# The gates' turn and spread moved from TensorE to VectorE block transposes and DMA reads, GELU in place in four PSUM banks

## The reference

```
h = layernorm(x) * (1 + ca) + sa
Q, K = elu(h Wq + bq) + 1, elu(h Wk + bk) + 1;  V = h Wv + bv        # 16 heads of 16
x = x + ga * (Q (K^T V) / (Q sum(K)) Wo + bo)
h = layernorm(x) * (1 + cb) + sb
logits = (h/|h|) . (centroids/|centroids|) + h . w_route              # 8 experts a token
gates  = softmax over the two largest logits, 0 for the other six
x = x + gb * sum_e gates[e] * (gelu(h w1[e] + b1[e]) w2[e] + b2[e])   # each expert 256 -> 128 -> 256
```

## Time and profile before

| | |
|---|---|
| median of three runs | 405.95 us |
| profiled execution: span from first to last instruction | 403.2 us (no other time of this execution is given; the median lies 2.75 us above it) |
| TensorE matmul busy | 377.8 us, 94% |
| TensorE weight load busy | 353.0 us, 88% |
| VectorE busy | 321.6 us, 80% |
| GpSimd busy | 285.1 us, 71% |
| ScalarE busy | 213.0 us, 53% |
| mean granted clock of TensorE | 0.987 of full |
| DMA | 13.44 MB, mean 33 GB/s |

### The profile page before, as it was taken

The page is one execution under the profiler, slowest core; times in us unless marked ns, Lnnn a source line. Parts: engine busy times, 40 slices in busy tenths (PEclk is TensorE's granted clock), DMA queues, the critical chain, the costliest instruction groups (busy, mean ns, idle before and its releaser), DMA issues.

```text
span 403.2 us, 9271 instructions
## 1 busy us (share of the span) xinstructions
PE 377.8 (94%) x2834; PEld 353.0 (88%) x2834; DVE 321.6 (80%) x880; ACT 213.0 (53%) x467; POOL 285.1 (71%) x263
## 2 busy tenths in 40 slices
PE   3999999999896759999999999999999999999995
PEld 3568889889775649999999999999999999999995
DVE  5998888888779887888888788888887888766644
ACT  2357877877552244453644644545545546455442
POOL 5426888788675768778878797797797877857410
PEclk9999999999999689999999999999999999999999
DMA  7954000000000000000000000000000000000000
GB/s 274 331 164 125 2 0 0 0 0 2 1 2 0 0 1 2 28 2 27 2 26 26 0 26 18 8 26 2 26 26 0 26 26 0 27 12 18 26 28 27
DMA packets 13706, 13.44 MB, mean 33 GB/s; under 512 B 1106, under 2 KB 12658, under 8 KB 13684
## 3 DMA queue, kind: packets, MB, share of 16 engines
q1 hardware_dynamic: 12868, 12.12, 9.6%
q10 hardware_dynamic: 816, 1.05, 0.8%
HBM read 8.98 MB, written 4.19 MB: 33 GB/s over the span
## 4 chain that ended last, share of the span: by engine, by line
PE 74%; DVE 11%; POOL 5%; issue 5%; DMA 2%; ACT 1%; SPq 0%; DVEq 0%; POOLq 0%
PE bank L698 19%; PE bank L700 19%; PE bank L699 18%; PE bank L706 4%; PE bank L909 3%; PE bank L762 2%; PE bank L869 2%; DMA x_sb<-in_x 2%; PE bank L877 2%; PE bank L927 2%; PE bank L730 2%; POOL hid_lo L470 1%; PE bank L795 1%; DVE stats L1034 1%; POOL early L443 1%
## 5 line engine op out<-in xcount | busy, mean ns | idle before, releaser
L470 POOL TENSOR_TENSOR hid_lo<-hid_g,hid_hi 128x512 fp32r<-128x512 f32 x56 | 72.1, 1288 | 39.9 <-ACT hid_hi L651 38.8
L642 ACT ACTIVATE hid<-bank,cols_sb 128x256 f32<-128x256 f32 x128 | 53.7, 470 | 76.7 <-PE bank L700 76.7
L698 PE MATMUL bank<-tr_hi,w_hi 128*128 128x256 f32 x256 | 73.6, 287 | 0.0
L698 PE MATMUL bank<-w_hi,hid_hi 128*128 128x256 f32 x252 | 71.5, 284 | 0.5 <-POOL hid_lo L470 0.5
L700 PE MATMUL bank<-tr_hi,w_lo 128*128 128x256 f32 x256 | 71.9, 281 | 0.0
L699 PE MATMUL bank<-tr_lo,w_hi 128*128 128x256 f32 x256 | 71.9, 281 | 0.0
L699 PE MATMUL bank<-w_lo,hid_hi 128*128 128x256 f32 x252 | 70.3, 279 | 0.0
L700 PE MATMUL bank<-w_hi,hid_lo 128*128 128x256 f32 x252 | 70.2, 279 | 0.0
L651 ACT ACTIVATE hid_hi<-hid_g 128x512 fp32r<-128x512 f32 x64 | 40.5, 632 | 44.0 <-DVE hid_g L1309 44.0
L1309 DVE TENSOR_TENSOR hid_g<-hid,bank 128x512 f32<-128x512 f32 x64 | 43.9, 686 | 21.8 <-ACT hid L642 21.5
L476 POOL TENSOR_TENSOR g_exp<-euler,shifted 128x16 f32<-128x16 f32 x16 | 49.2, 3077 | 5.2 <-DVE shifted L1342 4.6
(11 more groups left out here) (159 smaller groups left out, 989.3 us busy)
## 6 DMA issues: line engine op xcount, KB each, us to landing
x_sb<-in_x SPq DMA_DIRECT2D x16, 256.0 KB, 2.8
out<-x_sb SPq DMA_DIRECT2D x15, 256.0 KB, 2.1
early<-in_wmod ACTq DMA_DIRECT2D x2, 512.0 KB, 7.6
q_sb<-in_w SPq DMA_DIRECT2D x2, 512.0 KB, 6.5
q_sb<-in_w SPq DMA_DIRECT2D x1, 1024.0 KB, 9.5
q_sb<-in_wqkvT SPq DMA_DIRECT2D x1, 768.0 KB, 6.3
early<-in_wmod SPq DMA_DIRECT2D x1, 512.0 KB, 4.1
wo_sb<-in_woT SPq DMA_DIRECT2D x1, 256.0 KB, 7.5
```

The lines of the kernel that those rows point to most:

```text
L470: gp.tensor_tensor(hid_lo[:, s, :, :], hid_g[:, s, :, :], hid_hi[:, s, :, :].bitcast(F32), ALU.subtract).then_inc(e_hlo, 1)
L642: last = ac.activation(hid[:, s, j, :], bank[2 + s][:, 2 * P * j:2 * P * (j + 1)], ACT.Gelu, bias=b1_sb[:, e:e + 1])
L698: te.matmul(out_ap, l_hi, r_hi, start=start, stop=False)
```

## The change

The gates of unit u+1 no longer pass TensorE after `route`. Four VectorE block transposes (32 × 32 blocks) turn the logits inside bank 1, four more turn the finished gates from tokens on partitions to experts on partitions (`gT_f`, 32 partitions). SP writes the eight rows of gates (8 KB) to DRAM scratch `g_dram` and reads them back in two DMAs, each four experts' rows to all 128 partitions (512 KB to SBUF), into `g_bc`. VectorE multiplies the GELU's result, now left in its own PSUM bank, with `g_bc`. `first` uses four banks (2 to 5) instead of two, `hid_hi` and `hid_lo` get four buffers. Only the second largest's power is taken on GpSimd (2 values a partition instead of 16). Logit work tensors lie in PSUM. The centroids' norms are folded into the routing weights in phase A. The order of every engine's step is rewritten: `second(u, 2)` and `second(u, 3)` come in step u+1, `route(u+2)` comes last in step u.

```diff
@@ SP
+            def put_gates(u):
+                wait(sp, e_gT, u.count(1, 1))
+                sp.dma_start(g_dram[u.h, :, :], gT_f[3 * NE:4 * NE, u.h, :]).then_inc(g_put, 16)
+            def spread_gates(u, k):
+                if k == 0:
+                    wait(sp, g_put, u.count(16, 16))
+                wait(sp, e_mul, u.count(NP, 2 * k + 2 - NP))
+                of = g_dram[u.h, 4 * k:4 * k + 4, :].rearrange("(p j) n -> p j n", j=2)
+                sp.dma_start(g_bc[:, 2 * k:2 * k + 2, :, :], of.partition_broadcast(P)).then_inc(g_got[k], 16)
+            def step_e(u):
+                n = u.plus(1)
+                if n:
+                    put_gates(n)
+                    spread_gates(n, 0)
+                if u.plus(-1):
+                    store(u.plus(-1))
+                if n:
+                    spread_gates(n, 1)
@@ GpSimd: order of a step is now lo_e(u-1, 3), exp_gates(u+1), lo_e(u, 0), make_prod(u+4), lo_e(u, 1),
@@ lo_e(u, 2), add_experts(u-1), norm_e(u+2), rstd_e(u+3), make_qz(u+4)
             def norm_e(u):
+                gp.tensor_scalar(h_n2[:, u.h, :], h_n2[:, u.h, :], NORM_EPS2, None, ALU.max).then_inc(e_n2, 1)
...
             def exp_gates(u):
-                gp.tensor_tensor(g_exp[:, :, :].rearrange("p t e -> p (t e)"), euler[:, :],
-                                 shifted[:, :, :].rearrange("p t e -> p (t e)"), ALU.pow).then_inc(e_gexp, 1)
+                gp.tensor_tensor(second_by[:, :], top[:, :, 1], top[:, :, 0], ALU.subtract).then_inc(e_shift, 1)
+                wait(pool, e_shift, u.count(1, 1))
+                gp.tensor_tensor(g_second[:, :], euler[:, :], second_by[:, :], ALU.pow).then_inc(e_gexp, 1)
@@ ScalarE: gelu(0), hi_o, hi_hid(0), gelu(1), keep_gates(u+1), hi_hid(1), gelu(2), square(u+2), hi_hid(2),
@@ gelu(3), hi_e(u+2), hi_hid(3); keep_logits is gone
             def keep_gates(u):
-                wait(act, e_gTp, u.count(1, 1))
+                wait(act, e_gT, u.count(1, 1))
...
             def gelu(u, p):
-                wait(act, e_mul, u.count(NP, p - 1))
...
-                    last = ac.activation(hid[:, s, j, :], bank[2 + s][:, 2 * P * j:2 * P * (j + 1)], ACT.Gelu,
-                                         bias=b1_sb[:, e:e + 1])
+                    half = bank[2 + p][:, 2 * P * j:2 * P * (j + 1)]
+                    last = ac.activation(half, half, ACT.Gelu, bias=b1_sb[:, e:e + 1])
@@ TensorE (tp_logits, spread_gates, tp_gates are gone)
             def first(u, p):
-                wait(pe, e_gelu, u.count(NP, p - 1))
+                wait(pe, e_mul, u.count(NP, p + 1 - NP))
...
             def step_e(u):
+                first(u, 0); tp_o(u+3); first(u, 1); second(u-1, 2); attend(u+3)       # conditions at both ends left out
+                first(u, 2); second(u-1, 3); first(u, 3); tp_e(u+2); second(u, 0); second(u, 1); route(u+2)
@@ VectorE
             def gate(u, p):
-                wait(dve, e_gb, u.count(NP, p + 1))
+                wait(dve, g_got[p // 2], u.count(16, 16))
-                TT(hid_g[...], hid[...], bank[4 + s][:, :], ALU.mult)
+                TT(hid_g[...], bank[2 + p][:, :], g_bc[:, p, :, :], ALU.mult)
             def gates_a(u):
+                wait(dve, e_route, u.count(1, 1))
+                for q in range(4):
+                    last = ve.transpose(lg[32 * q:32 * (q + 1), :, :], by_quarter[:, :, q, :])
+                # then: cosine part times h_rn (128x32), a reduce to logit, ve.max per tile,
+                # first_of and second_of by is_ge; lg, logit, second_of, g_sel in bank 1
             def gates_b(u):
+                # per tile g_sel = max(second_of * g_second, first_of); reduce; reciprocal; two products
+                # to g_nat; one subtraction g_nat - g_nat
+                for q in range(4):
+                    last = ve.transpose(to, part.bitcast(F32))
+                last.then_inc(e_gT, 1)
             def step_e(u):
+                gates_a(u+1); gate(u, 0); lo_o(u+3); gates_b(u+1); gate(u, 1); modulate_e(u+2)
+                add_attention(u+3); gate(u, 2); scale_experts(u-1); stats_e(u+3); gate(u, 3)
+                denominators(u+4); lo_e(u+2)
@@ set-up: sel, sel_f, fold and their six instructions are gone; in phase A, step 1 of VectorE gets
+                if u.nth(1):
+                    split_b2()        # seven small instructions
+                    split_route()     # waits for GpSimd's cent_rn, three instructions
@@ passage
-            pe.wait_ge(cent_n2_ready, 1)       # tp_a of unit 14
```

More of the change, by code:

```diff
@@ L809, in _ @@
             mod_rows(1)
+            pe.wait_ge(cent_sq_ready, 1)
+            for c in range(NC):
+                last = te.matmul(bank[5][:, 0:NE], ones_f, cent_sq[:, c, :], start=(c == 0), stop=(c == NC - 1))
+            last.then_inc(cent_done, 1)
             pipeline(te, step_a, 1, 2, NU - 4, NU - 3)
@@ L822, in make_m @@
                 last.then_inc(f_m, 1)
-            pe.wait_ge(small_ready, 1)
             pe.wait_ge(a_hf, NU - 3)
-            for c in range(NC):
-                last = te.matmul(bank[0][:, E:E + NE], ones_f, cent_sq[:, c, :], start=(c == 0), stop=(c == NC - 1))
-            last.then_inc(cent_done, 1)
             sum_k(0, bank[0][:, 0:E])
@@ L900, in first @@
                 last.then_inc(e_f1, 1)
-            def spread_gates(u, p):
-                s = p % 2
-                if p == 0:
-                    wait(pe, e_gT, u.count(1, 1))
-                wait(pe, e_mul, u.count(NP, p - 1))
-                for j in range(2):
-                    last = te.matmul(bank[4 + s][:, 2 * P * j:2 * P * (j + 1)], sel[:, 2 * p + j, :], gT[:, u.h, :],
-                                     start=True, stop=True)
-                last.then_inc(e_gb, 1)
             def second(u, p):
-                s = p % 2
                 wait(pe, *lo_made(u, p))
@@ L951, in step_e @@
             def step_e(u):
-                n = u.plus(1)
-                if u:
-                    if not u.nth(0):
-                        first(u, 0)
-                    spread_gates(u, 0)
-                if u.nth(-1):
-                    route(n)
-                    tp_o(u.plus(3))
-                else:
-                    if u.plus(3):
-                        tp_o(u.plus(3))
-                    if n:
-                        route(n)
+                if u and not u.nth(0):
+                    first(u, 0)
+                if u.plus(3):
+                    tp_o(u.plus(3))
+                if u and not u.nth(0):
+                    first(u, 1)
+                if u.nth(-1):
+                    first(u.plus(1), 0)
+                if u.plus(-1):
+                    second(u.plus(-1), 2)
+                if u.plus(3):
+                    attend(u.plus(3))
+                if u.nth(-1):
+                    make_m(1, bank[7])
+                    first(u.plus(1), 1)
+                if u:
+                    first(u, 2)
                 if u.plus(-1):
@@ L990, in step_e @@
                 if u:
-                    second(u, 2)
-                if n:
-                    tp_gates(n)
+                    second(u, 0)
+                    second(u, 1)
+                if u.plus(2):
+                    route(u.plus(2))
             step_a(unit(NU - 2))
@@ new lines, in gates_a, with gates_b @@
+                wait(dve, e_top, u.count(1, 1))
+                TT(first_of[:, :, :], logit, top[:, :, 0:1].to_broadcast([P, 2, NE]), ALU.is_ge)
+                TT(second_of, logit, top[:, :, 1:2].to_broadcast([P, 2, NE]), ALU.is_ge).then_inc(e_gstep, 1)
+            def gates_b(u):
+                wait(dve, e_gstep, u.count(G, 3))
+                wait(dve, e_gexp, u.count(1, 1))
+                for t in range(2):
+                    last = ve.scalar_tensor_tensor(g_sel[:, t, :], second_of[:, t, :], g_second[:, t:t + 1],
+                                                   first_of[:, t, :], ALU.mult, ALU.max)
+                last.then_inc(e_gstep, 1)
```

422 lines of the change are left out of this document (188 added, 234 removed).

## The result

The changed kernel takes 414.76 us (median of four runs, 413.55 to 415.69) against 405.68 us for the kernel before beside it: ratio 1.0221, 95% interval 1.0186 to 1.0256. The forecast was 388.4 us, 378 to 402. The profiled execution has a span of 412.7 us and a time of 414.25, so 1.55 us lie outside the span (2.75 were counted).

What follows compares the result with a forecast made beforehand. VectorE's loop was taken as the bound at 15.1 us a step (3.0 + 9.5 + 2.65). 148.0 us ahead plus 237.6 for the steps and end gave a 385.6 span; with 2.75 added, 388.4 us, range 378 to 402.

Steps and rivals of the forecast that it cites:

- TensorE is the bound before: Steady step of the kernel before: TensorE is busy for all of its 16.01 us, so its list sets the step.
- TensorE's floor of 14.3 us: TensorE's list in a changed step: 16.01 less 1.68 us for gate spreads and the logits' and gates' turns.
- The loop `lo_e`, `route`, `gates_a`, ..., `lo_e`: From one lo_e's end to the next, VectorE's work and the wait for route set the step: 15.1 us.
- The transposes: VectorE's block transposes in gates_a and gates_b: 0.24 us each without overlap, 0.96 for four; bounds 0.12 and 0.38.
- `gates_b`, 2.65 us with blocking: VectorE's work from the two products per tile to the four gate transposes: 2.4 us, plus 0.25 blocking by GpSimd.
- rival (d): No difference: blocking on both comparisons and dear transposes together, 16.3 us a step or more, 403 us and up; chance 0.07.
- VectorE's step without gates, 9.5 us: Gate products, lo_o, add_attention, lo_e, modulate_e (1.6), scale_experts, statistics and denominators on VectorE sum to 9.5 us a step.
- Step 0 like the others: Step 0 was counted among steps 0 to 11 at 15.1 us each, 181.2 us in all.
- The end, 56.4 us: Steps 12 to 15 at 14.3, 12.5 and twice 11.6 us, last matmuls 2.8, then 3.9 to the end.
- Ahead of the steps, +0.3: Start-up, step 1 and passage up to lo_e(1): net +0.6 us, taken as +0.3, so it ends at 148.0.
- The DMAs: Put of the gates about 2.1 us; reads have 9.0 us of room, with 4.1 to 7.6 seen for 512 KB: both fit.
- The 2.75 us between span and median: The median time was taken to lie 2.75 us above the profiled span.

Runs made afterwards that it cites:

- experiment 10: The kernel before the change, with the gates spread over half of the tokens only (output not the reference's): 402.69 us, 0.9921 of the kernel before.
- experiment 12: Experiment 7 with the splits of b2 and of the centroids' columns moved from VectorE's step 1 to behind denominators(0): 390.73 us, 0.9630 of the kernel before.
- experiment 2: The changed kernel with lo_e ahead of denominators on VectorE: 409.63 us, 1.0096 of the kernel before.
- experiment 4: The changed kernel with the four transposes of gates_b done twice, once into a spare tile: 433.44 us, 1.0652 of the kernel before.
- experiment 8: The changed kernel with four more matmuls of 256 columns a step on TensorE: 415.23 us, 1.0236 of the kernel before.
- experiment 1: The changed kernel with modulate_e ahead of gate(u, 1) on VectorE: 417.39 us, 1.0278 of the kernel before.
- experiment 3: The changed kernel with modulate_e ahead of gate(u, 1) and lo_e ahead of denominators on VectorE: 406.42 us, 1.0009 of the kernel before.
- experiment 5: Experiment 3 with gelu(u, 2) ahead of hid_hi(u, 1) on ScalarE: 402.30 us, 0.9909 of the kernel before.
- Experiment 7: Experiments 5 and 6 together, with GpSimd's three add_bo spread over steps -1 and 0: 394.62 us, 0.9737 of the kernel before.
- Experiment 6: Experiment 3 with first(15, 0) ahead of second(14, 0), and scale_experts ahead of lo_hid(u, 2) in the last two steps: 399.99 us, 0.9865 of the kernel before.
- experiment 9: The changed kernel with each read of the gates issued twice, one after the other: 415.79 us, 1.0254 of the kernel before.
- experiment 11: Experiment 7 with make_qz ahead of rstd_e on GpSimd: 401.24 us, 0.9885 of the kernel before.

## Why the prediction was wrong

The spans differ by 412.7 - 385.6 = 27.1 us from the forecast's. By its own parts: `lo_e(1)` ended at 150.17 and not at 148.0 (+2.2); steps 0 to 11 took 196.4 us, from there to 346.55, and not 181.2 (+15.2); the rest took 66.15 us and not 56.4 (+9.8).

*TensorE is the bound before.* Right, by experiment 10.

*TensorE's floor of 14.3 us.* Nearly: 14.92 busy in the changed kernel, with its waits, and 14.46 in experiment 12, with few.

*The loop `lo_e`, `route`, `gates_a`, ..., `lo_e`.* Right in its mechanism, by the idles of 0.75 us on VectorE and 0.5 on TensorE once a step, and by experiments 2, 4 and 8. A second wait of TensorE, 0.7 us a step before `second(u, 0)`, was not foreseen; experiment 8 shows that it cost nothing in the steady step.

*The transposes.* Right: 0.24 us each in `gates_b`, 0.27 in `gates_a`, no overlap.

*`gates_b`, 2.65 us with blocking.* Right: 269.79 to 272.48, 2.69. The comparisons on the logits' bank were not blocked (0.17 us each), so rival (d), with blocking there and dear transposes, is not what happened, though the time came out where it put it. (Its condition was also mispriced: two comparisons at 1 us each are 15.1 + 2.0 - 0.2 = 16.9 us a step, not 16.)

*VectorE's step without gates, 9.5 us.* **This is the step that failed.** It took `modulate_e` as 1.6 us, as in the earlier trace rows, in a place where it now starts together with a GpSimd instruction that reads SBUF: 2.62 us. The forecast asked of every *new* instruction what GpSimd does beside it, and of no *moved* one. In the step shown that alone is the difference: forecast 3.0 + 9.5 + 2.65 = 15.15, measured 16.03 from end to end, of which +1.02 `modulate_e`, +0.16 the lead to the first gate, -0.3 the rest. Every second step is 0.5 us longer (16.52): its first gate waits 0.40 us for a GELU, and L1296 takes 0.60. Eleven steps at 16.24 instead of 15.1 are 12.5 of the 15.2 us, and `modulate_e` at 1.0 us each is 11.4 of them. Taking that microsecond away did not by itself give it back: experiment 1 gained nothing, the same move on top of experiment 2 gave 3.2 us (experiment 3), and only with the GELU moved too (experiment 5) was the step 15.12 us.

*Step 0 like the others.* It took 17.7 us (149.54 to 167.28), the other 2.6. A wait of 0.81 us for `g_second`, behind `add_bo`; L1296 at 1.31 and `neg_mean` at 1.02, both beside a GpSimd instruction, against 0.45 and 0.32 in the step shown above; and 1.16 instead of 0.75 us for `route`. TensorE's mean granted clock in this step was 0.72, in step 0 of the kernel before (147.06 to 162.18) 0.89; what that cost was not separated. Experiment 7 took the first wait away, and there the step lasted 15.05.

*The end, 56.4 us.* The second large miss, and not a cost but an omission: the forecast let TensorE run through. (Its parts, 14.3 + 12.5 + 23.2 + 2.8 + 3.9, are 56.7, a slip of 0.3.) Step 13 lasted 14.22 us where 12.5 was forecast, with TensorE busy for 12.49 of them: 1.7 of the 9.8. Most of the rest lies behind `lo_e(15)`, where TensorE stood idle for 38.0 - 29.8 = 8.2 us. In the waits from 375 us on stands

```profile
PE bank L862 <- DVE k_sb L1313: 4.2, 2, 3.2
```

`second(14, 0)` waits for `scale_experts(13)`, which the new order puts behind `lo_hid(u, 2)`; `first(15, 0)` stands behind both `second`s of unit 14, so ScalarE and VectorE then wait 5.0 and 5.2 us for it. The forecast named `scale_experts` only by its duration. Experiment 6 took 6.4 us off the time, 4.3 of them seen in this stretch. The end also ran at a granted clock of 0.95, against 1.00 in the kernel before; what that cost was not separated.

*Ahead of the steps, +0.3.* `lo_e(1)` came 2.5 us later than in the kernel before. Three distances on VectorE divide this. Its first statistics of phase A start 0.9 us earlier (24.82 against 25.75). From there to the next ones it takes 13.20 us (to 38.02) instead of 8.62 (to 34.37), 4.6 longer: the work that came back in step 1 took 3.15 us (34.87 to 38.02), and `ga_bo` ahead of it 1.49 instead of 0.41. From there to `lo_e(1)` it is 1.2 us shorter, where the forecast had 0.3 lost. The forecast charged 1.6 us for the work that came back; by experiment 12, moving it away saved 2.2. That is 0.6 of the miss of 2.2 us, and the rest stays open: experiment 8, whose code is the same up to there, has its `lo_e(1)` at 150.82 and not at 149.54.

*The DMAs.* Right, with more room than counted: the put landed within 1.4 us (2.1 counted), the reads in 3.8 us (bounds 4.1 and 7.6), and experiment 9 found no cost beyond 1.0 us in twice that. Issues of the changed kernel, to be read beside the earlier trace rows:

```profile
g_bc<-g_dram SPq DMA_DIRECT2D x32, 512.0 KB, 3.8
...
out<-x_sb SPq DMA_DIRECT2D x15, 256.0 KB, 2.3
```

The Trainium skill (DMA: Bandwidth & Descriptors, Latency and other measured facts) led, by its 103 GB/s for copies whose rows lie 4 or 8 MiB apart, to an estimate of 7.1 us for such a read; 128 partitions reading one place of 4 KB were not that case, and took 3.8.

*The 2.75 us between span and median.* It was 1.55 in the profiled run, 1.2 us less than counted, which hid as much of the miss.

So the mechanism, the new parts and the arguments against the rivals were right, and the sum was wrong in the main by work that was only moved and by waits at both ends. Its range, too, was made from the unknown durations alone, and held nothing for blocking in moved work, for step 0 or for the waits of the end.

## What to carry to other kernels

- When an order is rewritten, price the moved instructions again in their new places: list what GpSimd does beside each VectorE instruction with both inputs in SBUF. Durations from the old place hold only for the old neighbours, and a later move shifts the neighbours again, as in experiments 5 and 12.
- A first and a last step have another order of waits than the steady one: follow each engine's list there from wait to wait, not by counts of matmuls.
- When a fix of one wait gives nothing, look for the wait that took its place before the theory is dropped: experiment 1 gave nothing, but the same move together with ScalarE's order took 7.3 us off experiment 2 (409.63 to 402.30).
- Look at all the times of a program before its profile is read for the median: the profiled execution of experiment 2 was 4.8 us below it.

## What the runs showed of the hardware

- A VectorE pair with both inputs in SBUF that starts together with a GpSimd subtraction of 512 columns: 1.91 us for 0.87, and the subtraction 1.59 for 1.29. The two losses together (1.04 and 0.30) are about the subtraction's own duration.
- A VectorE transpose of 32 partitions by 64 float32 values, neighbours on different quarters: 0.24 us from SBUF to SBUF, 0.27 within a PSUM bank, one after the other.
- A matmul of 128 columns behind others of 256 costs 0.085 us where one of 256 costs 0.115: halving the columns saved a quarter.
- A VectorE subtraction of 16 columns within SBUF: 0.18 us alone, up to 1.33 beside a GpSimd instruction (experiment 11).
- Two programs with the same steady code and another start differ by 0.22 us a step (experiments 7 and 12).
